# Windowed attention: the sixth of eight score blocks (number 7) masked by selections on GpSimd in place of a mask product on TensorE

## What is computed

```python
local = _local_attention(heads(q), heads(k), heads(v))      # 16 heads of 8, blocks of 128 queries, window 128
allowed = (dist > 0) & (dist <= w) & (k_gpos >= 0)
scores = jnp.where(allowed, scores, NEG)                    # then softmax and the product with v
...
lat_out = softmax(where(lat_allowed, rq @ rk, NEG)) @ rv    # 4 heads over 64 pooled latents
mixed = gate * local + (1.0 - gate) * remote_h
return mixed @ out_w + out_b
```

## Time and profile before

| what | us |
|---|---|
| median of 3 runs | 551.62 |
| lowest and highest run | 549.55, 555.9 |
| profiled execution, its own time | 553.63 |
| its span, first to last instruction | 551.8 |
| around the span (553.63 less 551.8) | 1.83 |

### The profile page before, as it was taken

The page is one execution under the profiler, slowest core; times in us unless marked ns, Lnnn a source line. Parts: engine busy times, 40 slices in busy tenths (PEclk is TensorE's granted clock), DMA queues, the critical chain, the costliest instruction groups (busy, mean ns, idle before and its releaser), DMA issues. The chain is left out here.

```text
span 551.8 us, 16727 instructions
## 1 busy us (share of the span) xinstructions
PE 506.1 (92%) x5277; PEld 312.0 (57%) x5280; DVE 428.4 (78%) x2018; ACT 297.2 (54%) x820; POOL 326.9 (59%) x735
## 2 busy tenths in 40 slices
PE   8978579999999999999999999869999999999991
PEld 3434224565666565565665665535677577677671
DVE  5986586899999999999999898635657677685655
ACT  2655305788888888788888888512211211312110
POOL 4799302688888888588888789841113333333241
PEclk9999855999999999999999999988999999999996
DMA  4465460324213323222332000000000000000001
GB/s 127 132 221 174 150 109 2 100 66 97 46 32 61 83 63 64 45 36 64 64 64 58 10 4 4 2 1 0 1 1 1 21 20 0 19 20 0 20 19 39
DMA packets 49059, 28.10 MB, mean 51 GB/s; under 512 B 6808, under 2 KB 48056, under 8 KB 48976
## 3 DMA queue, kind: packets, MB, share of 16 engines
q1 hardware_dynamic: 47648, 26.73, 19.7%
q10 hardware_dynamic: 1328, 0.36, 0.3%
HBM read 17.90 MB, written 8.91 MB: 49 GB/s over the span
## 5 line engine op out<-in xcount | busy, mean ns | idle before, releaser
L1097 DVE CUSTOM_DVE_ANT_0 added<-psS,maskq 128x256 bf16<-128x256 f32 x512 | 199.8, 415 | 25.4 <-PE psS L938 18.5
L1325 ACT ACTIVATE probs<-psST 128x512 f32<-128x512 f32 x240 | 143.4, 598 | 37.5 <-PE psST L974 35.3
L974 PE MATMUL psST<-qst,kst 50*128 50x128 bf16 x992 | 101.1, 222 | 0.0
L938 PE MATMUL psS<-kst,qst 48*128 48x256 bf16 x448 | 91.7, 287 | 2.3 <-DVE rowmax L1097 1.3
L1769 ACT ACTIVATE hT<-fpsH 128x512 f32<-128x512 f32 x32 | 19.2, 599 | 121.6 <-PE fpsH L1513 121.6
L995 PE MATMUL psPV<-probs,vst 128*10 128x128 f32 x1984 | 80.1, 277 | 3.1 <-issue 0.6
L1242 POOL TENSOR_SCALAR_AFFINE_SELECT probs<-probs 128x256 f32<-128x256 f32 x150 | 62.0, 414 | 5.2 <-ACT probs L1325 5.0
L1245 POOL TENSOR_SCALAR_AFFINE_SELECT probs<-probs 128x256 f32<-128x256 f32 x150 | 62.6, 417 | 0.0
L938 PEld LDWEIGHTS psS<-kst,qst 48*128 48x128 bf16 x448 | 25.2, 95 | 62.4 <-issue 39.5
L974 PEld LDWEIGHTS psST<-qst,kst 50*128 50x128 bf16 x992 | 55.9, 95 | 0.0
L1510 PE MATMUL fpsH<-xehi,w1hi 128*128 128x512 f32 x128 | 55.7, 435 | 0.0
(11 more groups left out here) (198 smaller groups left out, 1078.8 us busy)
## 6 DMA issues: line engine op xcount, KB each, us to landing
q_parts<-early SPq DMA_DIRECT2D x8, 384.0 KB, 2.6
k_parts<-early SPq DMA_DIRECT2D x8, 384.0 KB, 2.7
qst<-q_parts SPq DMA_DIRECT2D x32, 96.0 KB
kst<-k_parts SPq DMA_DIRECT2D x32, 96.0 KB
X<-in_L_attn_x_dram SPq DMA_DIRECT2D x8, 256.0 KB, 3.2
qst<-q_parts SPq DMA_DIRECT2D x32, 64.0 KB
kst<-k_parts SPq DMA_DIRECT2D x32, 64.0 KB
out_dram<-res SPq DMA_DIRECT2D x8, 256.0 KB, 2.3
```

Source lines behind the costliest of these rows:

```text
L938: last = nc.tensor.matmul(bank[:, a], q, kst[rows, slot, ring(n - 1, 2)], start=True, stop=True)
L974: last = nc.tensor.matmul(bank[:, a, side * P:(side + 1) * P], kst[rows, slot, ring(n - 1 + side)], qst[rows, slot, ring(n)], start=not ma ...
L1097: taken = nc.vector.tensor_tensor_reduce(added[:, 2 * (g % 2) + a], psS[g % 2][:, a], mask, 1.0, NEG * 4, ALU.add, ALU.max, rowmax[:, n.mo ...
L1325: nc.scalar.activation(probs[:, g ^ 1], psST[g % 2][:].rearrange("p a c -> p (a c)"), ACT.Exp, scale=SCALE).then_inc(s_exp.sem, 1)
```

## The change

Block 7 joins `SELECTED`, and GpSimd's list gets one more `select` behind that of block 6. `s_sel` now counts six events in a step, and values(3) waits for the sixth. In the 30 steps that select, `mask_t` is no longer issued for block 7, and each of its score products into psST starts and ends by itself.

```diff
-SELECTED = (0, 2, 3, 4, 6)
+SELECTED = (0, 2, 3, 4, 6, 7)
...
                     select(s, SELECTED[4])
+                    select(s, SELECTED[5])
                 if (s - 3).live:
```

## The result

The changed kernel takes 564.82 us (median; runs from 562.95 to 565.42), the kernel before 550.59 in the same measurement. The ratio is 1.0235, 95% interval 1.016 to 1.0309: slower; whether by more than 2%, the interval leaves open. The profiled execution took 565.05 us with a span of 563.2; before it was 553.63 and 551.8. So the span is 11.4 us longer.

A forecast was written before the change was run, and what follows sets the result against it. GpSimd's loop from lprob over block 3's selections and values(1) was taken to bound the kernel. Terms 6.3 + 2.3 + 1.1 + 1.5 + 0.6 = 11.8 us on 551.62 gave 563.4, plus 2.1%; range 557.5 to 569.

The forecast's parts named there:

- What bounds the kernel: A loop of waits through GpSimd, values(1), block 6's scores, their maximum and lprob, summing to the 8.13 us half step.
- The 0.14 ahead of values(1): Time from block 3's selections on GpSimd to values(1) on TensorE, taken as a wait of 0.14 us, not slack.
- the stretch: GpSimd from lprob's start to the end of block 3's selections in the next step: 6.25 us in a half step.
- the two chains: The GpSimd loop and a chain over block 7's scores and VectorE, said to balance at 8.13 us each.
- The part removed: 30 mask products of block 7 on TensorE: alone worth up to 0.24 us a step, entered as nothing.
- the first rival: Pair fits GpSimd's idle time and the mask product was on the path: 6.7 us off, 544.9; chance 0.06.
- Half steps: Two windows with 14 half steps: loop lengthens to 8.60 us a step, 120.40 for 114.10, plus 6.3.
- Full steps: Loop of 8.73 us: seven steps plus 2.3, five more plus 1.1; 0.40 of the 0.73 hidden by TensorE's work.
- The last two steps: GpSimd busy 18.00 of 18.59 us, nothing hides a pair: 2 x 0.73, plus 1.5.
- After the last lprob: One pair ahead of X and yrstd, less yrstd's idle 0.16: plus 0.6 us.
- The waits don't add up: New wait of 0.40 us at values(3) not added to that at values(1); rival: they add, 573.5, chance 0.09.
- VectorE's idle time: Sign in the changed profile: VectorE's idle time would grow; no size given.

The follow-up runs named there:

- E2: Kernel before, block 7's product kept, plus a pair of selections on a spare tile behind block 6's that no engine waits for: 563.84 us, ratio 1.0203.
- E3: Kernel before with the same spare-tile pair placed behind block 4's selections, ahead of diff: 552.89 us, ratio 1.0017.
- E1: Kernel before without block 7's mask product and without selections for it, so part of the computation is missing: 545.53 us, ratio 0.9873.
- E8: Kernel before with GpSimd's residual addition X and yrstd moved ahead of diff up to step 29, block 7's product kept: 552.19 us, ratio 1.0.
- E6: Changed kernel with GpSimd's residual addition X moved ahead of diff up to step 29: 559.45 us, ratio 1.0126.
- E11: Changed kernel with values(3) issued behind block 2's scores instead of block 1's: 564.39 us, ratio 1.0215.
- E5: Changed kernel, but in steps 30 and 31 block 7 keeps its mask product and has no pair: 562.52 us, ratio 1.0177.

## Why the prediction was right

The forecast was 563.4 us, plus 11.8 on 551.62; measured are 564.82 and a ratio of 1.0235, and the span grew by 11.4.

- **What bounds the kernel: right for the changed kernel, too strong for the one before.** The 0.14 ahead of values(1) was no slack. E2 and E3 show it most plainly: the same pair inside the stretch costs 2.0% and behind it nothing that can be measured. But the two chains of the kernel before did not balance. E1 leaves GpSimd's list alone and its steps are 0.20 shorter, and E8 takes work out of the stretch and its steps stay at 8.13. So a path over block 7's product held the step, and yrstd's wait inside the GpSimd stretch only filled the time. Whether that path was the one through VectorE or TensorE's own list, which has no listed wait in that half step, no run parts. Without that wait GpSimd's loop was shorter than the step; an estimate from the changed kernel's steps is 8.49 - 0.73 = 7.76 in a half step and 8.70 - 0.73 = 7.97 in a full one. So 0.37 of the pair in a half step and 0.43 in a full one filled slack, and only the rest was paid.
- **The part removed: right in kind.** E1 gives 0.20 us in a half step, for "up to 0.24", and 545.53 us in all, near the 544.9 of the first rival. In the changed kernel it is worth nothing: E2, which keeps all products, has the same step lengths within 0.03. So the expected gain exists and is shut out by a longer loop.
- **Half steps: a little too long.** The loop was put at 8.60 and is 8.49. The stretch is 6.61, not 6.72: when yrstd's wait ends, more than its listed 0.26 of idle time goes. Its start came 0.49 behind that of L1262 and comes 0.18 behind it now. The term was 6.3 and is 2.20 + 2.48 = 4.68; 14 x 0.11 = 1.5 of the difference is the shorter loop. The second of the 14 intervals did not grow at all (8.14 before, 8.13 now).
- **Full steps: right.** The loop was put at 8.73 and is 8.70. The terms 2.3 and 1.1 are 2.77 and 1.56; two steps of the first full window (8.97 and 9.06) are longer for other reasons, as some were before.
- **The last two steps: too low.** 1.5 was entered and 2.97 measured. The doubling that I weighed and left out of the sum happened: by the Trainium skill, SBUF — State Buffer, section "Who interferes with whom", a VectorE instruction with two SBUF inputs contends with a GpSimd instruction that reads SBUF, and the trace agrees with 0.85 and 0.94 us for a selection beside such an instruction and 0.40 for one beside none. No run varied this alone. What I didn't see was the clock behind it. E2, with the same pair but no wait, loses 1.49 and keeps the clock at 1.00. The other 1.48 are the wait and the clock together, and no run parts them.
- **After the last lprob:** 0.6 entered, 0.27 measured.
- **The sum: partly luck.** The last two steps took 1.5 more than entered, the half steps 1.6 less. The full steps took 4.33 for 3.4, 0.9 more, and the 0.89 by which the changed kernel was ahead before the first window takes that back. Nothing in the change explains this 0.89: in the experiments the same step comes anywhere from 98.27 to 103.35. The total is nearer than its parts.
- **The waits don't add up: right.** values(3) waits 0.32 (0.40 was worked out), values(0) 0.29 and values(1) 0.17, and the step is only as long as the one loop. E6 then shows the limit of it: with 0.41 out of the stretch, the loop over values(3) is the next one, and in full steps only 8.70 - 8.55 = 0.15 of the 0.41 is won.
- **VectorE's idle time: half right.** It was to grow. In the first window of half steps it did, from 56.84 - 52.94 = 3.90 to 59.04 - 54.39 = 4.65; in the first of full steps it fell, from 58.77 - 53.87 = 4.90 to 61.54 - 57.12 = 4.42.

No version was found that beats the kernel before with all of the work in it.

## What to carry to other kernels

Where several engines are nearly full and run by fixed lists, follow one step's loop of waits and add up its parts until they give the step's length. Work put inside that loop costs its length less the slack that the loop still has (0.36 of 0.73 us here in a half step), and the same work a few places away in the same list, outside the loop, can be free. A constant distance of 0.14 us between the end of one engine's work and the start of another's can be a wait that the list of waits doesn't name. Before taking work off a busy engine, ask which loop is the next longest, and how much slack it has, since a wait inside a loop can hide that slack: a product's removal was worth 1.3% alone and nothing beside a longer GpSimd stretch.

## What the hardware showed that was not expected

TensorE's granted clock fell after an idle time of 1.82 us in an attention step: 1.00 in the window with the idle time, 0.55 in the one behind it, although TensorE was busy for 3.40 of its 3.40 us, and then back to 1.00. Short waits in every step didn't do it: the steady steps wait 0.32, 0.29 and 0.17 us, TensorE is busy for 92% of them (54.37 of 59.04 us), and the clock is 1.00. E6 has a wait of 1.83 us in its last steps, and 0.81 and 0.85 in the two windows of 5 us around and behind it. E11 has one of 1.60 us, and the clock falls there too:

```profile
356.58 0.99 PE L995 MATMUL psPV<-probs,vst 128*10 128x128 f32 x16 [1.60 <-POOL probs L1244]
...
356.65:358.65 2.00, 2.00 (x21) 1.56 (x21) 0.95 (x2) 0.60 (x1) 2.00 (x5) 0.51 0.04 12
358.65:360.65 2.00, 2.00 (x25) 0.99 (x24) 1.24 (x3) 0.38 (x1) 1.49 (x4) 0.64 0.00 0
```

The longest idle times ahead of values in the last steps of E2 and E5 are 1.35 and 0.89 us, and their clock stays at 1.00. So one late buffer cost twice: once as the wait, and once in the slower work behind it. That the idle time caused the fall is read from this order of events, and no run changed the idle time alone. It need not come in every execution: E6's four had mean granted clocks of 0.950, 0.944, 0.959 and 0.959 and took 560.92, 563.02, 557.98 and 557.72 us, and only the first was profiled.

GpSimd's selections went from 0.41 to 0.85 and 0.94 us beside VectorE instructions of the weight preparation with two inputs in SBUF, while the mean over all 180 of one line stays at 0.414.
